# Attention and recurrent feed-forward block on one core: tail keys once per batch, normalisations on ScalarE, two banks for the first projections

## What is computed

```python
x = x + attention(layernorm(x))      # x: (32, 256, 128)
x = x + ffn(layernorm(x))

def attention(x, norm_weight, w_qkv, w_out, persist_mem):
    h = rms_norm(x, norm_weight)
    q, k, v = split(h @ w_qkv.T)                   # 16 heads of 64 each
    q, k = rope(q), rope(k)
    k = concatenate([persist_mem, k]); v = concatenate([persist_mem, v])   # 260 keys
    scores = q @ k.T / 8, causal: key j <= query i + 4
    return (softmax(scores) @ v) @ w_out.T

def ffn(x, wf, uf, bf, wi, ui, bi, wc, uc, bc, wo, uo, bo, in_c):
    for xt in x:                                   # over the 32 batches
        c = sigmoid(xt @ wf.T + c @ uf.T + bf) * c \
            + sigmoid(xt @ wi.T + c @ ui.T + bi) * tanh(xt @ wc.T + c @ uc.T + bc)
    return tanh(x @ wo.T + c @ uo.T + bo)          # the last c, for all batches
```

## Time and profile before

| | |
|---|---|
| median of 3 runs | 1224.16 us (1223.3 to 1224.5) |
| the profiled execution's own time | 1220.81 us |
| its span | 1218.9 us |
| PE busy | 1155.1 us, 95% of the span |
| PE weight loads | 858.2 us, 70% |
| DVE busy | 991.7 us, 81% |
| POOL busy | 631.9 us, 52% |
| ACT busy | 624.2 us, 51% |
| DMA | 121.48 MB, mean 100 GB/s |
| TensorE clock granted | 0.988 of full, mean |

### The profile page before, as it was taken

How to read it: one execution, slowest core, us unless ns; L and a number is a source line. 1 busy time by engine, 2 the same in 40 slices (tenths; PEclk the granted TensorE clock), 3 DMA queues, 4 the chain that set the end, 5 groups by cost and what they waited for, 6 DMA issues and landing times.

```text
span 1218.9 us, 38148 instructions
## 1 busy us (share of the span) xinstructions
PE 1155.1 (95%) x13867; PEld 858.2 (70%) x13867; DVE 991.7 (81%) x3428; ACT 624.2 (51%) x1316; POOL 631.9 (52%) x953
## 2 busy tenths in 40 slices
PE   3889999999999999999999999999999999999991
PEld 1557777777777777777777777777777777777771
DVE  5877888888888888888888888888888898887746
ACT  2645555555555555554555554554555555555533
POOL 2545555555555555555555455554555555555415
PEclk9989999999999999999999999999999999999996
DMA  5322333333233333323333322333322333332114
GB/s 176 109 87 88 100 104 108 106 109 100 76 103 104 104 107 108 94 74 106 106 107 108 108 87 77 106 104 102 113 89 83 103 100 104 102 104 87 58 37 138
DMA packets 77996, 121.48 MB, mean 100 GB/s; under 512 B 13041, under 2 KB 34930, under 8 KB 77682
## 3 DMA queue, kind: packets, MB, share of 16 engines
q1 hardware_dynamic: 76338, 116.42, 31.6%
q10 hardware_dynamic: 1472, 2.62, 0.6%
HBM read 43.10 MB, written 8.78 MB: 43 GB/s over the span
## 4 chain that ended last, share of the span: by engine, by line
PE 70%; DVE 16%; DMA 5%; issue 4%; SPq 2%; ACT 1%; POOL 1%; DVEq 0%; POOLq 0%; ACTq 0%
PE bank_pv L1008 12%; PE bank L920 11%; PE bank_st L971 10%; PE bank_sum L1042 8%; PE bank_sum L1025 6%; DVE masked L715 5%; PE bank L934 5%; PE bank_sm L948 4%; DMA rope_c<-rope_b 3%; PE bank_st L974 2%; PE bank L1128 2%; PE bank L1130 2%; PE bank_sum L1031 1%; DVE c_lo L807 1%; PE bank_sm L956 1%
## 5 line engine op out<-in xcount | busy, mean ns | idle before, releaser
L375 POOL TENSOR_TENSOR qk<-rope_a,rope_c 128x512 f32<-128x512 f32 x256 | 332.8, 1300 | 271.5 <-DMA rope_c<-rope_b 263.1
L715 DVE CUSTOM_DVE_ANT_0 masked<-bank_sm,mask_q 128x132 bf16<-128x132 f32 (+1 forms) x1024 | 307.6, 356 | 41.6 <-PE bank_sm L948 40.8
L505 ACT ACTIVATE prob<-bank_st 128x776 f32<-128x776 f32 x256 | 208.5, 815 | 166.1 <-PE bank_st L974 165.2
L704 DVE TENSOR_TENSOR rope_a<-bank,cos 128x512 f32<-128x512 f32 x256 | 174.2, 680 | 108.1 <-PE bank L920 104.6
L366 POOL TENSOR_SCALAR_AFFINE_SELECT prob<-prob 128x256 f32<-128x256 f32 x256 | 115.6, 452 | 273.3 <-ACT prob L505 273.3
L971 PE MATMUL bank_st<-qk 64*128 64x256 f32 (+1 forms) x2048 | 240.3, 327 | 0.0
L1008 PE MATMUL bank_pv<-prob,v_sb 128*64 128x256 f32 (+1 forms) x2048 | 224.9, 340 | 0.1
L490 ACT ACTIVATE qk_h<-qk 128x512 f16<-128x512 f32 x256 | 159.5, 623 | 90.6 <-POOL qk L375 90.6
L971 PEld LDWEIGHTS bank_st<-qk 64*128 64x128 f32 x2048 | 155.0, 188 | 31.8 <-issue 1.1
L1008 PEld LDWEIGHTS bank_pv<-prob,v_sb 128*64 128x64 f32 x2048 | 124.4, 136 | 70.8 <-issue 31.1
L705 DVE TENSOR_TENSOR rope_b<-bank,sin 128x512 f32<-128x512 f32 x256 | 173.8, 679 | 0.0
(11 more groups left out here) (188 smaller groups left out, 1796.3 us busy)
## 6 DMA issues: line engine op xcount, KB each, us to landing
rope_c<-rope_b SPq DMA_DIRECT2D x512, 128.0 KB, 2.1
rinv<-linv_scratch SPq DMA_DIRECT2D x124, 256.0 KB, 4.6
out<-x_sb SPq DMA_DIRECT2D x16, 256.0 KB, 2.5
linv_scratch<-linv SPq DMA_DIRECT2D x62, 64.0 KB, 2.1
x_sb<-x SPq DMA_DIRECT2D x29, 128.0 KB, 2.9
v_end<-v_end_scratch SPq DMA_DIRECT2D x64, 32.0 KB
pre<-w_qkv_t ACTq DMA_DIRECT2D x1, 1024.0 KB, 5.4
v_sb<-pm_v SPq DMA_DIRECT2D x64, 8.0 KB
```

The costliest lines, as they stand in the source:

```text
L375: G.tensor_tensor(qk[:, s, :].rearrange("p (u n) -> p u n", u=2)[:, :, 0:NT], rope_a[:, s % 4, :].rearrange("p (u n) -> p u n", u=2), rope ...
L505: A.activation(prob[:, s % 4, :, :], ps_st[:, :, 0:SCOL], ACT.Exp).then_inc(S["exp_done"], 1)
L704: V.tensor_tensor(rope_a[:, s % 4, :], ps_proj[:, :], cos[:, :], ALU.mult)
L715: ins = V.tensor_tensor_reduce(masked[:, e, c0:c0 + n], ps_sm[:, e, c0:c0 + n], mask_q[:, c0:c0 + n], 1.0, LOWEST, ALU.add, ALU.max, top[: ...
```

## The change

- **Tail keys.** `attend` has no tail matmuls for pairs 0 to 6. For pair 7 two matmuls with 32 columns (8 pairs x 4 queries) make the tail's part of all pairs in free columns of `ps_pv`. `v_end` is now 128 wide and holds the four pairs of each half on their own partitions. DVE's new `end_add` adds this part to `raw` before `divide`, and `attend(bj, 0)` of the next batch waits for it. `prob_end` is doubled. SP's load of `v_end` moves from `tails` (s = 3 and 6) to `tail_values` at s = 5. In `sums` the tail's 2 matmuls of 128 weight columns become 4 of 32, each on its own quarter of the columns, the same shape as the rest of `sums`.
- **Normalisations.** `first_norm` and `second_norm` move from DVE to ScalarE (2 activations each, with scale and bias per partition); POOL's `factors` and `rstd` get two more small products each for the bias. `c_hi` is made on ScalarE (`state_high`, s = 5) and not on DVE. `divide` and `c_lo` become `scalar_tensor_tensor` in place of `tensor_tensor`.
- **Start.** In iteration 0 the projections s = 1 and 3 go to `ps_work` and may run one ahead of `rotate`. ScalarE casts `w_qkv` ahead of the wait for `ld_ident`, and the loads of the feed-forward and output weights are issued after both. `end_values` moves from iteration 0 to s = 0 and 1 of iteration 1, `end_low` from s = 1 to s = 5 of iteration 0.
- **Loads of x.** `load_batch` moves from SP's queue to ScalarE's, at s = 4.

```diff
@@ attend
                 for kc, q0, c0 in CHUNKS:
                     for e in range(2):
                         col = (2 * s + e) * DH
-                        T.matmul(ps_pv[OWN[e], q0:NT], v_sb[:, kc, col:col + DH], prob[:, s % 4, e, c0:c0 + NT - q0],
-                                 start=(kc == 0), stop=False)
-                for e in range(2):
-                    col = (2 * s + e) * DH
-                    last = T.matmul(ps_pv[OWN[e], QE:NT], v_end[:, col:col + DH], prob_end[:, e, s, :],
-                                    start=False, stop=True)
+                        last = T.matmul(ps_pv[OWN[e], q0:NT], v_sb[:, kc, col:col + DH], prob[:, s % 4, e, c0:c0 + NT - q0],
+                                        start=(kc == 0), stop=(kc == 1))
+                if s == NPAIR - 1:
+                    pe.wait_ge(S["v_end"], 32 * (bj + 1))
+                    pe.wait_ge(S["end_exp"], 2 * bj + 2)
+                    for e in range(2):
+                        last = T.matmul(ps_pv[OWN[e], NT:NT + NPAIR * NEND], v_end[:, e * DH:e * DH + DH],
+                                        prob_end[:, bj % 2, e, :, :].rearrange("p s n -> p (s n)"), start=True, stop=True)
@@ sums
-                    for e in range(2):
-                        last = T.matmul(ps_sum[:, QE:NT], ones_end[:, e, :], prob_end_sum[:, e, :],
-                                        start=False, stop=(e == 1), skip_group_check=True)
+                    for r in range(4):
+                        last = T.matmul(ps_sum[32 * r:32 * r + 32, QE:NT], ones_end[:, r % 2, 32 * r:32 * r + 32],
+                                        prob_end_sum[:, r % 2, :], start=False, stop=True, skip_group_check=True)
@@ vector engine, s == 1, after rotate
+            def end_add(cj, par):
+
+                dve.wait_ge(S["raw_done"], NPAIR * cj + NPAIR)
+                o = raw[:, par, :, QE:NT]
+                V.scalar_tensor_tensor(o, ps_pv[:, NT:NT + NPAIR * NEND].rearrange("p (s n) -> p s n", s=NPAIR), 1.0 / RS, o,
+                                       ALU.mult, ALU.add).then_inc(S["end_added"], 1)
@@ scalar engine, s == 7, after raw_copy
+            def second_norm(cj):
+
+                act.wait_ge(S["sx_rstd"], cj + 1)
+                wait(act, S["xt_ready"], cj)
+                for q in range(QT):
+                    last = A.activation(xn[:, q * D:(q + 1) * D], at3s(x_sb, cj, q * D, (q + 1) * D), ACT.Identity,
+                                        bias=sx_m[:, q:q + 1], scale=sx_r[:, q:q + 1])
+                last.then_inc(S["xn_ready"], 1)
@@ GpSimd, rstd
                 G.tensor_tensor(sx_b[:, :], sx_mv[:, :, 1], eps[:, 0:QT], ALU.add).then_inc(S["pool_b"], 1)
-                pool.wait_ge(S["pool_b"], cj + 1)
-                G.tensor_tensor(sx_r[:, :], sx_b[:, :], expo[:, 0:QT], ALU.pow).then_inc(S["sx_rstd"], 1)
+                wait(pool, S["xn_ready"], cj)
+                G.tensor_tensor(sx_m[:, :], sx_mv[:, :, 0], minus[:, 0:QT], ALU.mult).then_inc(S["pool_b"], 1)
+                pool.wait_ge(S["pool_b"], 3 * cj + 2)
+                G.tensor_tensor(sx_r[:, :], sx_b[:, :], expo[:, 0:QT], ALU.pow).then_inc(S["pool_b"], 1)
+                pool.wait_ge(S["pool_b"], 3 * cj + 3)
+                G.tensor_tensor(sx_m[:, :], sx_m[:, :], sx_r[:, :], ALU.mult).then_inc(S["sx_rstd"], 1)
@@ tensor engine, project
-                wait(pe, S["qk_read"], NPAIR * j + s)
+                wait(pe, S["qk_read"], NPAIR * j + s - (1 if j == 0 and s < 5 else 0))
```

188 lines of the change are left out of this document (101 added, 87 removed).

## The result

The changed kernel takes 1207.61 us (median of 4 runs, 1204.28 to 1210.63), the kernel before 1224.33 beside it. The ratio is 0.9864, 95% interval 0.9829 to 0.9899: 16.6 us less, where 32.0 were forecast, and 0.6 us above the end of the range. The profiled execution is the fastest of the four, 1204.28 us with a span of 1202.5 (1218.9 before).

What follows compares the result with a forecast made beforehand. PE was taken to bound every iteration. The terms -15.7 - 12.5 + 1 - 3.5 - 2 + 0.7 sum to -32.0 us, taking the median from 1224.16 to 1192.2 us, with a range of 1181 to 1207.

Steps and rivals of the forecast that it cites:

- What bounds the kernel: Whole run: PE, busy 95% of the span, sets the pace in every iteration; other engines have 5 to 17 us spare.
- Tail of `attend`: Pairs 0 to 6: 224 groups lose 0.07 us each, the change-of-shape cost of 0.10 staying: -15.7 us.
- rival A: Tails of attend and sums: the whole slot goes, a change of shape costing nothing; -57.6, 1166.6 us; chance 0.06.
- Tail of `sums`: Last part of sums, once per batch: 0.87 us in place of 1.26, over 32 batches -12.5 us.
- Pair 7: attend's remaining tail, 32 columns in place of 4: 0.03 us more per batch, +1 us.
- What PE saves shortens the run nearly one to one: Whole run: shortening PE's list shortens the run by nearly as much, as long as no other engine becomes late.
- rival B: Each iteration: PE faster but other engines late, 0.4 us waiting each, 12.8 us back; 1205 us; chance 0.14.
- The seam: Between iterations: ScalarE's normalisation just in time for PE's transpose, about 0.1 us of wait left: -3.5 us.
- rival C: Step 7: ScalarE waits for POOL's late factor and PE behind it; slower than before, 1240 us; chance 0.04.
- Moved loads: Loads of x and v_end leaving SP's queue at s = 3 and 4: costed at nothing.
- Start: Before iteration 1: earlier casts and work off the path start iteration 1 some 3.5 us earlier; -2 us together.
- End: Last normalisation, alone on the final chain: POOL's two products add about 0.5, c_hi 0.2: +0.7 us.

Runs made afterwards that it cites:

- tail_only: Kernel before with only the tail keys' edits (attend, sums, exp, end_sum, end_add, tail_values): 1201.83 us, ratio 0.9827.
- tail_norms: tail_only plus both normalisations and the state's high part on ScalarE, with POOL's products with -1: 1206.43 us, ratio 0.9853.
- tail_loads: tail_only plus the loads of x issued by ScalarE's queue: 1209.01 us, ratio 0.9880.
- loads_sp: Changed kernel with the loads of x back on SyncE's queue: 1204.70 us, ratio 0.9845.
- tail_start: tail_only plus the new start alone: 1202.58 us, ratio 0.9827.
- start_old: Changed kernel with the start of the kernel before: 1209.61 us, ratio 0.9886.
- after_late: Changed kernel with the transpose of xn behind scores_for_max in step 0: 1208.47 us, ratio 0.9883.
- tail_inv2: tail_only with VectorE's reciprocal ahead of the rotation of step 1: 1203.50 us, ratio 0.9844.
- mid_inv: tail_only with xn's transpose between the last attend and last part of sums, its readers moved too, and the reciprocal ahead of step 1's rotation: 1216.16 us, ratio 0.9932.
- tail_half: tail_only with the second half of the rinv loads issued behind the swap of the following step: 1201.93 us, ratio 0.9824.
- tail_late: tail_only with the transpose of xn behind scores_for_max in step 0: 1204.29 us, ratio 0.9851.
- mid2: tail_only with xn's transpose between the last attend and last part of sums, xt_high right behind exp, xt_low behind first_stats: 1195.65 us, ratio 0.9763.
- norms_dve: Changed kernel with both normalisations and the state's high part back on VectorE, without POOL's products with -1: 1207.10 us, ratio 0.9865.
- mid2_start: mid2 with the change's new start: 1193.86 us, ratio 0.9767.

## Why the prediction was wrong, step by step

32.0 us were forecast and 16.6 measured. Of the missing 15.4, about 6 went between PE's shorter list and the run, about 6 with the normalisations (forecast -2.8 with the end, measured +3.2), and the rest with the loads of x, costed at nothing, and the start.

- **What bounds the kernel**: right. PE set the pace, and the shortest iteration shrank by just what its list lost.
- **Tail of `attend`**: right in mechanism and nearly in size. 0.81 and not 0.80 with 0.87 before: 224 x 0.06 = -13.4 where -15.7 was forecast. The change of shape stayed, as promised, and rival A fell.
- **Tail of `sums`**: 0.83, forecast 0.87: 32 x -0.43 = -13.8 where -12.5 was forecast. **Pair 7**: 0.90 - 0.87 = +0.03 per batch, +1 us, as forecast. The three together -26.2 for -27.2.
- **"What PE saves shortens the run nearly one to one"** is the step that failed. Of 0.84 us per iteration tail_only keeps 0.60. Step 0 loses 0.12 of it (its wait grew from 0.37 to 0.49 us, since PE comes sooner to the transpose and VectorE does not), step 6 another 0.12 (five long ones became nine). 26 iterations of 0.24 make 6.2 us, and that is most of what separates tail_only's 21 from 27.2. This is rival B, at a smaller rate than its 0.4, in two places. By the prediction's own test, over 0.3 us of waiting per iteration, B is proved in the whole change too: 14.3 us in 31 waits are 0.46. I had read the waits as small in the whole-span list, but that list does not say how far behind the next one is. For the divided values I had also read PE's row alone, 1.9 us; the row of its weight loads in the same list had 5.5 us in 10 waits, and has 9.0 in 18 after the change.
- **The seam**, forecast -3.5: wrong by the price of one operation. The start of ScalarE's normalisation (0.27 behind `raw_copy`) came as worked out. POOL's factor came 0.09 us ahead of it and not 0.5, but it held ScalarE up only three times, 6.9 us of which 5.98 at the end, so rival C fell. The pair of activations took 0.87 us and not 0.61, 488 ns each where the row that I took has 361, and PE waits 0.26 us in every iteration: just the difference. VectorE's pair took 0.60. The forecast had given a bound of "each takes 0.1 longer", and each took 0.13. The row that I took has one operand per partition, the scale; the normalisation has two and reads SBUF. In the same trace `gate_tanh` of 128x256 with a bias per partition takes 474 ns and `raw_copy` of 128x256 without one 371, so the second operand may be most of the difference; it was not tried alone. What VectorE's way had besides, a step 0 without a wait in a third of the iterations, went as well. tail_norms against tail_only: +3.2 us by the ratios; in the two profiled runs, which lie 6.8 us apart, 2.6 are in the middle (35.25 for 35.15 us per iteration) and 3.2 at the end.
- **Moved loads**, forecast at nothing: +6.5 us alone (tail_loads), +2.3 beside the rest (loads_sp against the changed kernel, at intervals that overlap). How they cost it is open in part, as said above. I had asked what else SP's queue carries, and not what the load passes when it leaves it.
- **Start**, forecast -2 with iteration 1 3.5 us earlier: the first projection is 1.5 us earlier, iteration 1 only 1.2, since `end_low` late in DVE's list holds `values` for 2.54 us. In time it is worth between 0 (tail_start) and 2.7 us (start_old). The clock did rise for good later, as one bound had it (41 us instead of 28), but iteration 0 grew by 0.3 us only; what the clock alone cost is not shown.
- **End**, forecast +0.7: 3.2 us against tail_only in the profiled runs. The rows show 0.6 to 0.7 us of ScalarE's and POOL's longer way twice, not once, and about 1.1 with the clock at half. Between runs with nearly the same clock up to 1.5 us are left for the change. Why the clock fell sooner is open; after_late, which has the same normalisations and 4.9 us at half, takes 1.7 less.
- **`end_add`, the wait of `attend(bj, 0)` for it**, at nothing: right (0.5 us in the whole span) until the reciprocal is put in front of it (0.16 us per iteration in tail_inv2, more in mid_inv).

The parts do not add up exactly: -21.2 + 3.2 + 6.5 + 0 = -11.5 for a measured -16.6. Each has an error of 2 to 3 us, and the loads cost less beside the other parts than alone. Not tried apart: `divide` as `scalar_tensor_tensor`, and `c_hi` on ScalarE without the normalisations.

## What to carry to other kernels

When the engine that sets the pace gets less work, look for the waits that are already at its edge, and ask by how much each grows if the engine comes sooner and nothing else does; a wait met in two iterations out of three is not 9 us in total but a wall. Price an operation by a row of the same operands (source memory, scale and bias per partition), not by one of the same size. A transfer that leaves a queue no longer waits behind what was in front of it: write down what it now runs ahead of. And before moving work into a gap of TensorE, look at the shapes of its two neighbours.

## What the runs showed of the hardware

- An activation of 128x128 f32 with scale and bias per partition, from SBUF to SBUF, took 488 ns on ScalarE (mean of 64; two in 0.87 us), one from PSUM to fp16 with a scale alone 361 ns; the same normalisation on VectorE took 0.60 us for two at the seam.
- A swap of 256 KB in two DMAs was issued 2.6 to 3.6 us behind the first of four loads of 256 KB, and POOL's instruction that waits for it started 4.8 to 6.4 us after its issue (tail_only, iterations 5 to 30). With only two of the four loads ahead of it, issued 1.4 to 2.7 us behind the first, it was 2.8 to 4.2 us (tail_half).
- A full-height transpose between two half-height groups cost 0.35 to 0.42 us more than right behind a full-height one (tail_late, tail_only); between two full-height groups with other column counts it cost 0.15 us more (mid2).
- TensorE's clock at the start: in the kernel before the matmuls of 256 columns went from 0.42 to 0.27 us, half to full clock, at 28 us, behind a dense stretch of projections and `end_values` (24.3 to 28.6 in the earlier trace rows and the rows around it), and in start_old at the same place. Without `end_values` there, and with PE waiting between the projections, it stayed at half until 38.9 us in norms_dve and 39.2 in mid2_start. In the changed kernel it was full from 17.4 to 20.8 us and then at half until 41.3; in tail_start and loads_sp it was full twice for 3.4 us and at half between and behind, until 40.7 and 38.8.
